# One stage chain of a graph kernel rebuilt: the switch (top-1 expert) layer on rows kept in SBUF, and longer edge loops

## The reference, cut to what matters

```
x = x + gnn1(layernorm(x))          # attention over 212500 edges, sorted by destination
h = layernorm(x)                    # 12500 x 256
probs = softmax(h @ gate_w + gate_b)            # 8 experts
idx, prb = argmax(probs), max(probs)
pos = (cumsum(one_hot(idx)) * one_hot(idx)).sum(-1) - 1
kept = pos < C                                  # C = ceil(1.25 * T / 8)
y = relu(h @ w1[idx] + b1[idx]) @ w2[idx] + b2[idx]   # 256 -> 1024 -> 256, for kept rows
x = x + nan_to_num(y * prb * kept, nan=0, posinf=1e4, neginf=-1e4)
```

## Time and profile before

| what | value |
|---|---|
| runs | 8990.95, 8987.5, 8998.53 us; median 8990.95 |
| the profiled execution's own time | 8983.79 us |
| its span | 8982.1 us |
| busy share of the span | PE 75%, DVE 61%, POOL 50%, ACT 49% |
| granted TensorE clock, mean | 0.867 |

### The profile page before, as it was taken

How to read it: one execution, slowest core, us unless ns; L and a number is a source line. 1 busy time by engine, 2 the same in 40 slices (tenths; PEclk the granted TensorE clock), 3 DMA queues, 4 the chain that set the end, 5 groups by cost and what they waited for, 6 DMA issues and landing times. The chain is left out here.

```text
span 8982.1 us, 148420 instructions
## 1 busy us (share of the span) xinstructions
PE 6727.8 (75%) x33082; PEld 4837.0 (54%) x33082; DVE 5448.7 (61%) x13922; ACT 4381.8 (49%) x12756; POOL 4468.3 (50%) x4428
## 2 busy tenths in 40 slices
PE   3888888888888887349757887877887833399980
PEld 1556666666666655347644555555555533266650
DVE  3469999999999987641165666666666653000009
ACT  0257777777777753224325666666666511022220
POOL 3046666666666650540076777777777600400007
PEclk6999999999999998569977888889888855699995
DMA  4466666666666663543473444444444454411115
GB/s 144 160 173 180 180 177 183 179 183 181 178 184 180 182 156 116 186 154 120 126 248 106 108 108 108 108 108 108 107 108 108 97 174 141 132 54 57 58 39 159
DMA packets 794356, 1248.35 MB, mean 139 GB/s; under 512 B 251754, under 2 KB 574692, under 8 KB 793102
## 3 DMA queue, kind: packets, MB, share of 16 engines
q0 software_dynamic: 271680, 827.74, 33.8%
q1 hardware_dynamic: 517283, 395.33, 15.0%
q10 hardware_dynamic: 4608, 16.78, 0.5%
HBM read 1003.93 MB, written 254.83 MB: 140 GB/s over the span
## 5 line engine op out<-in xcount | busy, mean ns | idle before, releaser
L694 POOL DMA_INDIRECT att_kv<-kv,att_idx x1872 | 1868.7, 998 | 1314.2 <-issue 859.9
L694 POOL DMA_INDIRECT gat_att_vst<-ft,gat_att_idx x1872 | 1838.7, 982 | 608.7 <-issue 532.8
L772 PE MATMUL gat_att_pag<-gat_att_msg,gat_att_S 128*128 128x260 f32 x3744 | 1219.7, 455 | 132.6 <-DVE gat_att_msg L977 127.6
L772 PE MATMUL att_pag<-att_msg,att_S 128*128 128x264 f32 x3744 | 1094.8, 416 | 177.5 <-DVE att_msg L977 162.9
L730 PE MATMUL att_pqd<-sum_acc,att_ST 128*128 x3744 | 1000.3, 391 | 18.1 <-ACT att_ST L816 4.7
L772 PEld LDWEIGHTS gat_att_pag<-gat_att_msg,gat_att_S 128*128 128x128 f32 x3744 | 741.6, 220 | 380.1 <-DVE gat_att_msg L977 226.0
L772 PEld LDWEIGHTS att_pag<-att_msg,att_S 128*128 128x128 f32 x3744 | 642.5, 191 | 485.8 <-DVE att_msg L977 343.6
L730 PEld LDWEIGHTS att_pqd<-sum_acc,att_ST 128*128 128x128 f32 x3744 | 709.6, 194 | 148.5 <-issue 45.8
L961 DVE TENSOR_TENSOR att_prod<-att_kv,att_pqd 128x512 f32<-128x512 f32 x936 | 642.8, 687 | 152.4 <-issue 51.7
L816 ACT CAST gat_att_ST<-gat_att_pST 128x256 bf16<-128x256 f32 x936 | 348.2, 372 | 699.1 <-PE gat_att_pST L707 668.4
L2377 POOL DMA_INDIRECT combine_yg<-ybuf,combine_slot x98 | 181.8, 1856 | 1018.7 <-DVE combine_slot L2387 989.2
(11 more groups left out here) (449 smaller groups left out, 12335.7 us busy)
## 6 DMA issues: line engine op xcount, KB each, us to landing
att_kv<-kv,att_idx POOLq DMA_INDIRECT x1872
gat_att_vst<-ft,gat_att_idx POOLq DMA_INDIRECT x1872
top_row<-tok SPq DMA_DIRECT2D x106, 256.0 KB, 2.8
ytok<-top_y SPq DMA_DIRECT2D x106, 256.0 KB
kv<-qkv_row SPq DMA_DIRECT2D x50, 520.0 KB
buf<-switch_zero ACTq DMA_DIRECT2D x32, 512.0 KB
experts_w<-in_L_ffn_w_dram SPq DMA_DIRECT2D x16, 1024.0 KB
experts_row<-buf SPq DMA_DIRECT2D x32, 512.0 KB
```

The lines of the kernel that those rows point to most:

```text
L694: pool.indirect_dma_start(row, None, rows_t, IndirectOffsetOnAxis(ap=idx[:, k, 2 * p + i:2 * p + i + 1], axis=0)).then_inc(s_g[p % R], 16)
L772: t = pe.matmul(pag[p % 2][:, 0:AW], S[:, gs % RG, 2 * p + i, :], msg[:, p % 2, i, :], start=(i == 0), stop=(i == 1))
```

## The change

1. edge_phase: UN goes from 6 to 18 steps in the loop's body, and 8 steps instead of 2 are written out ahead of it (6 passes instead of 19).
2. add_rows, node_tables "gate_ln" and moe_switch are no longer called. In their place stand three stages.
   - switch_route: for each of 14 groups, DVE divides acc, adds x into acc (x is loaded once, and never stored back), takes the statistics and normalises into a ring of rows with 4 more columns; PE turns the rows and multiplies by the gate; DVE finds the expert and its probability, PE cumulates the counts, DVE computes the slot and writes the row's weight (probability, or 0 beyond the capacity) into column 256 of the row; POOL scatters the 7 blocks to stok. At the end POOL scatters 16 blocks of zeros behind the experts' rows, and DVE makes the table of the tiles.
   - switch_experts: 56 tiles of 256 rows (14336 rows). The weights of a tile's expert (2.1 MB) are loaded for every tile, into a ring of 3. The weight, the NaN and infinity replacement are applied here, on 512 elements a partition.
   - switch_out: POOL gathers the rows of sy (98 indirect DMAs), DVE adds them into acc (once a group), SP stores the output.

```diff
@@ edge_phase
-    UN = 6
+    UN, HEAD = 18, 8
...
-            assert (NG - 3) % UN == 0
-            for g in range(2):
+            assert (NG - 1 - HEAD) % UN == 0
+            for g in range(HEAD):
                 step(g, g)
-            with eng.Fori(0, (NG - 3) // UN) as it:
+            with eng.Fori(0, (NG - 1 - HEAD) // UN) as it:
                 for j in range(UN):
-                    step(it * UN + (2 + j), 2 + UN + j)
+                    step(it * UN + (HEAD + j), HEAD + UN + j)
@@ graph_program
-            phase(add_rows, c, dr, acc, 4)
-        phase(node_tables, c.ident, "gate_ln", dr["x"], [(0, a["L1_ffn_gate_w"])], 8, dr["logits"], ln_out=dr["ln"])
-        moe_switch(nc, c, dr, a["L1_ffn_gate_b"], a["L1_ffn_w1"], a["L1_ffn_b1"], a["L1_ffn_w2"],
-                   a["L1_ffn_b2"], out)
+            d = Switch(s)
+            phase(switch_route, c, dr, d, acc, a["L1_ffn_gate_w"], a["L1_ffn_gate_b"])
+            phase(switch_experts, c, dr, d, a["L1_ffn_w1"], a["L1_ffn_b1"], a["L1_ffn_w2"], a["L1_ffn_b2"])
+            phase(switch_out, c, dr, d, acc, out)
@@ switch_route, DVE and POOL, for each group
+                divide(0)
+                add(0)
+                stats(0)
+                divide(1)
+                norm(0)
+                for g in range(NGR):
+                    if g + 1 < NGR:
+                        add(g + 1)
+                        if g + 2 < NGR:
+                            divide(g + 2)
+                        stats(g + 1)
+                    if g == 0:
+                        v.wait_ge(s_w, 32)
+                    scores(g)
+                    if g + 1 < NGR:
+                        norm(g + 1)
+                    best(g)
+                    places(g)
...
+                for g in range(NGR):
+                    pool.wait_ge(s_slot, g + 1)
+                    pool.sem_inc(s_go, 1)
+                    for k in range(K):
+                        b = g * K + k
+                        pool.indirect_dma_start(dr["stok"], IndirectOffsetOnAxis(ap=d.slot[:, b:b + 1], axis=0),
+                                                ln[:, g % R, k, :], None).then_inc(s_sc[g % R], 16)
@@ switch_experts, SP
+                def weights(i):
+                    e, s = load_value(d.tile_e, i, 7), i % WR
+                    of = lambda a: a[bass.ds(e, 1)]
+                    sp.dma_start(W1[:, s, :, :], of(w1).rearrange("e (c p) n -> (e p) c n", p=P)).then_inc(s_w[s], 16)
+                    sp.dma_start(B1[:, s, :], of(b1).rearrange("e (c p) -> (e p) c", p=P),
+                                 allow_slow_non_contiguous=True).then_inc(s_w[s], 16)
+                    sp.dma_start(W2[:, s, :, :], of(w2).rearrange("e (c p) n -> (e p) c n", p=P)).then_inc(s_w[s], 16)
+                    sp.dma_start(B2[:, s, :], of(b2).to_broadcast([P, D])).then_inc(s_w[s], 16)
...
+                for i in range(TILES):
+                    sp.wait_ge(s_y, i + 1)
+                    if i + WR < TILES:
+                        weights(i + WR)
+                    if i + R < TILES:
+                        rows(i + R)
+                    sp.dma_start(dr["sy"][i * T2:i * T2 + T2, :].rearrange("(k p) d -> p k d", p=P),
+                                 y[:, i % YR, :, :]).then_inc(s_ys[i % YR], 16)
@@ switch_experts, PE
+                turn(0)
+                turn(1)
+                hidden(0)
+                for i in range(TILES):
+                    if i + 2 < TILES:
+                        turn(i + 2)
+                    if i + 1 < TILES:
+                        hidden(i + 1)
+                    result(i)
@@ switch_out
+                    for k in range(K):
+                        b = g * K + k
+                        pool.indirect_dma_start(yg[:, g % R, k, :], None, dr["sy"], IndirectOffsetOnAxis(
+                            ap=d.place[:, b:b + 1], axis=0)).then_inc(s_g[g % R], 16)
...
+                    v.wait_ge(s_g[g % R], (g // R + 1) * K * 16)
+                    a = acc[:, g * K:g * K + K, 0:D]
+                    v.tensor_tensor(a, a, yg[:, g % R, :, :], ALU.add).then_inc(s_add, 1)
```

More of the change, by code:

```diff
@@ new lines, in switch_out, with _ @@
+def switch_out(nc, c, dr, d, acc, out):
+    K, R = 7, 4
+    NGR = NBLK // K
+    s_g = sems(nc, "sout", *[f"gathered{r}" for r in range(R)])
+    s_add, s_st, s_go = sems(nc, "sout", "added", "stored", "go")
+    with Scope(nc, "sout") as m:
+        yg = m.sb("yg", [P, R, K, D])
+        with nc.Block() as block:
+            @block.gpsimd
+            def _(pool):
+                for g in range(NGR):
+                    if g >= R:
+                        pool.wait_ge(s_add, g - R + 1)
+                        pool.sem_inc(s_go, 1)
+                    for k in range(K):
+                        b = g * K + k
+                        pool.indirect_dma_start(yg[:, g % R, k, :], None, dr["sy"], IndirectOffsetOnAxis(
+                            ap=d.place[:, b:b + 1], axis=0)).then_inc(s_g[g % R], 16)
+            @block.vector
+            def _(v):
+                for g in range(NGR):
+                    v.wait_ge(s_g[g % R], (g // R + 1) * K * 16)
+                    a = acc[:, g * K:g * K + K, 0:D]
+                    v.tensor_tensor(a, a, yg[:, g % R, :, :], ALU.add).then_inc(s_add, 1)
+            @block.sync
+            def _(sp):
+                for g in range(NGR):
+                    sp.wait_ge(s_add, g + 1)
+                    r0, b0 = g * K * P, g * K
+                    whole = min(K, N // P - b0)
+                    sp.dma_start(out[r0:r0 + whole * P, :].rearrange("(k p) d -> p k d", p=P),
+                                 acc[:, b0:b0 + whole, 0:D]).then_inc(s_st, 16)
+                    if whole < K:
+                        sp.dma_start(out[r0 + whole * P:N, :], acc[0:N - r0 - whole * P, b0 + whole, 0:D]).then_inc(s_st, 16)
+                sp.wait_ge(s_st, 16 * (NGR + 1))
@@ L2433, in graph_program @@
               flag=dram("flag", (4, NS)), kv=dram("kv", (NR, D + 264)), ft=dram("ft", (NBLK * P, 260)),
-              logits=dram("logits", (NR, 8)), ln=dram("ln", (NR, D)), buf=dram("buf", (8 * 2048, D)),
-              ybuf=dram("ybuf", (8 * 2048, D)), tok=dram("tok", (8 * Dispatch.CAP, D)),
+              ln=dram("ln", (NR, D)), stok=dram("stok", (8 * Switch.CAP, Switch.W)),
+              sy=dram("sy", (Switch.TILES * 2 * P, D)), tok=dram("tok", (8 * Dispatch.CAP, D)),
               ytok=dram("ytok", (Dispatch.TILES * 2 * P, D)))
```

734 lines of the change are left out of this document (400 added, 334 removed).

## The result

The changed kernel takes 8470.26 us (median of 4 runs, 8461.98 to 8473.22), the kernel before 8989.23 beside it: ratio 0.9422, 95% interval [0.9408, 0.9436]. The forecast was 8428, its range 8350 to 8540. The profiled execution has a span of 8471.5 us.

The account below looks back on a forecast made before the run. It took PE to bound the experts stage, and transfers, serial chains, POOL and DVE the other rebuilt stages. Route 279, experts 839, out 149 and 1 made 1268 for 1782; with the loops -562, so 8428 us, range 8350 to 8540.

Parts of the forecast that it names:

- the likeliest case: Whole kernel: the forecast itself, 8428 us, own range 8380 to 8470, chance 0.60.
- Loops: Edge loops: 18 back jumps become 5 in each phase, saving 48 us in att and 0 in gat_att.
- I take 3.7: att loop: us saved for each of 13 back jumps removed, chosen between 2.9 and 4, giving 48 us.
- Rival 4: Edge loops: longer bodies cost as much as they save, by dearer jumps or slow fetch; +48, 8476 us; chance 0.04.
- Route: switch_route: start 36, 13 groups 208, last scatters 8.9, zeros 20.3, landing and barrier 6; 279 us.
- I take 16.0 a group: switch_route: us for each group of 7 blocks, between 14.4 without waits and 19.8 as in top2_route.
- Experts: switch_experts: 15 us until the first product, 56 tiles at 14.5, 12 at the end; 839 us for 972.4.
- L = 9.4: switch_experts: us for a tile's weights to be issued and land, 2.23 MB at 307 GB/s plus register read and latency.
- V: switch_experts: DVE's work on one tile with the hand-over, before SP issues the weights; 5.7 us.
- The forecast's own upper bound: switch_experts: bound of L from the whole 11.2 us up to 7915 plus 0.6; V + L 17.5, 15.7 us a tile.
- rival 2: switch_experts: weights set the pace; V + L of 18.2, 16.0 us a tile, 8512 us, up to 8650; chance 0.22.
- Out: switch_out: 98 gathers at 1.26 us, 12 lost beside DVE's additions, plus start and end; 149 us for 241.8.

Follow-up runs that it names:

- e1: The kernel before with only the new edge loops (bodies of 18 steps, 8 ahead): 8960.61 us, ratio 0.9964.
- e2: The changed kernel with the old edge loops (bodies of 6 steps, 2 ahead): 8518.73 us in one run.
- e3: The changed kernel without the NaN and infinity replacement in the experts stage (6 of DVE's 8 operations a tile): 8386.13 us.
- e4: The changed kernel with weights and biases loaded for the first three tiles only: 8387.75 us.
- e5: The changed kernel with SP issuing the next row tile before the weights: 10110.93 us in one run, on the second chip (kernel before 10603.66).
- e6: The changed kernel with W1, B1 and W2 issued ahead of DVE's wait, after PE's last product: 9995.65 us, second chip (kernel before 10603.66).
- e9: The changed kernel again, unchanged, on the third chip: 8485.74 us, ratio 0.9427 to the kernel before.
- e11: The changed kernel with edge loops written out and weights issued ahead of DVE's wait, third chip: 8371.95 us, ratio 0.9306.

## Why the prediction was right, and where it was off

The range holds 8470.26 and the sign was right, but the time lies at the very edge of the likeliest case's own range, 8380 to 8470. Of the four terms the loops brought less and the experts cost more than forecast; route and out cost a little less, so that 22 us of error cancel by luck.

- *Loops, forecast -48, measured -26 in att (-34 in all, e1).* Two steps failed. "I take 3.7" a jump was too much: the 23.37 us a group that it is measured against came from 3 groups, and straight code takes 2724.4 / 116 = 23.5. Against that a jump costs 2.75, so 13 fewer are worth 36. And the cost of one jump was taken to stay: it about doubled (4.7 to 5.6 us), and by the packets on q8, as I read them, because PE's body is fetched again. Rival 4 named a dearer jump with a factor of 3; the factor is 2. That gat_att would gain nothing is true of the pair before and after (2 us), but not of all runs (some 10 us, see e2).
- *Route, forecast 279, measured 262.5.* "I take 16.0 a group": it was 14.9, from the slots of the groups (7204.8 to 7398.3, 13 periods). The first scatter came after 34.6 us (36 forecast). The term that was too large is DVE's own work: it is busy for 156.8 us in these 13 periods, 12.1 a group for 14.4. The waits were there: 1.2 us a group for the positions (16.9 in 14 times), 8.0 us for logits, but in 2 groups only, and the rest in gaps of a few tenths between its operations. The clock stayed at 0.50 there, as said.
- *Experts, forecast 839, measured 894.1.* The step that failed is L = 9.4. V was right (5.7; from 7800.43 to 7805.9, and the hand-over). But the transfer that PE waits for is not the weights but the rows behind them on SP's queue, and L for these is about 11: they leave 5.7 us after DVE's end, with SP held some 3 us at the bias, and land 5 us later. So V + L is 16.95 for 15.1. The hold stood in the trace of before (3.63 us). The forecast's own upper bound, which took the whole stretch up to 7915 with the row tile in it, gave 15.7 a tile, and that is nearly what came. The form of the sum, (V + L + PE's tile) / 2, fits e3: its V + L of about 12.7 lies below PE's 14.25, and PE's pace is what it shows. e4 fits likewise; neither tests more than the floor. PE's own floor, forecast 14.3, was exact. What the sum has no term for is that PE runs 14 us slower in all by the waits (814.5 for 800.7 busy). The measured 15.6 lies nearer to rival 2's 16.0 than to the forecast's 14.5: what SP issues behind DVE's wait sets the pace, as rival 2 said, though through the rows and not through the weights that it named. Had route and out not come out 22 us cheaper, the time would have been 8492, still inside the range.
- *The Trainium skill's price for a DMA* (the Trainium skill, "DMA: Bandwidth & Descriptors", Anatomy of one DMA) would have given L = 7.7 and no wait. The page fits it to single DMAs issued by GpSimd, and these are issued by SP, four or five on one queue at one moment. The runs show 58 us of wait in the run of tiles, and here the measurement decides.
- *Out, forecast 149, measured 143.6.* 98 gathers have a mean of 1.066 us for 0.946 alone: 11.8 us lost beside DVE's 28.4, where 12 was forecast. The loss falls on 13 gathers of 1.77 to 1.92 us, one for each addition that has a gather beside it, as the prediction said ("0.95 us, or 2 under an addition"):

```profile
L2553 POOL DMA_INDIRECT sout_yg<-sy,sum_place x98 | 104.5, 1066 | 928.8 <-PEq L2543 899.2 <-issue 29.6
```

## What to carry to other kernels

When a load is hung behind one engine's "done", list everything that queue issues behind the wait and cost the last item, not the largest one, and look how long each issue holds the queue; then ask what each buffer really waits for, since an earlier releaser (here PE's last read, not DVE's last write) may take the whole chain off the path for one moved wait: 72 to 78 us here. In such a chain two small cuts need not be worth two gains: e3 and e4 each reach the engine's floor alone, so nothing is left there for the other. And a wait of an engine near full use can cost more than its length, here 72 us for 58.

A longer loop body is not a shorter version of the same cost. Count what each jump costs from a trace of straight code, and look whether the long body is still held by every engine: in att 12 steps were worth nothing, 18 steps half of what was hoped for, and straight code 26 us more.

## What was not expected of the hardware

- A back jump over a body of 12 or 18 steps costs 4.7 to 6.7 us against 2.75 to 2.9 for one of 6, and the granted clock is at 0.50 for about 10 us behind it, where behind a jump over 6 steps it is there for 3 to 7 us or not at all.
- SP's issue of the fourth load of a burst (W1, bias, W2, broadcast bias) took 3.16 us (median), in e5 4.69, in the kernel before 3.63 (one expert), and 0.35 when the three ahead had been issued 4 us earlier (e6). What it waits for, no trace says.
- The same program, the kernel before, took 10603.66 us on one chip and medians of 8989 to 9002 elsewhere. In the traces from that chip the edge phases are longer, and so are two stages in the middle: the scatters of top2_route take 332 us from first to last in e6 (276 in e9), the gathers of gat_tables 322 (251). Others are not: switch_route's scatters take 201 us on both, and the experts stage of e6 is 821.7 us, that of e11 elsewhere 822.4. The edge phases show stalls of all engines together; their cause was not found.
